# Who rounds and who takes the turned weight units in the last batch of a one-core decoder layer

## The chip, the cores and the metric

The kernel runs on one core of a Trainium2 chip. A core has TensorE (PE, with its weight loads shown apart as PEld), VectorE (DVE), ScalarE (ACT), GpSimd (POOL), SyncE (SP, whose queue here only starts transfers), one SBUF, one PSUM and 16 DMA engines. The metric is the device time of one execution in microseconds. One execution was also taken with the hardware profiler; times inside it are microseconds from the start of its span.

## The reference

One decoder layer with three parts, each added to its input: a linear self-attention, a cross-attention over 750 context rows, and a feed-forward part with ternary weights and 8-bit activations. x is 8 x 224 x 512, the context 8 x 750 x 512, and the feed-forward matrices are 2048 x 512 (gate, up) and 512 x 2048 (down).

```python
def _weight_quant(w):
    scale = 1.0 / jnp.clip(jnp.mean(jnp.abs(w)), 1e-05)
    wq = jnp.clip(jnp.round(w * scale), -1.0, 1.0) / scale
    return w + jax.lax.stop_gradient(wq - w)
def _bitlinear(x, w):
    return jnp.einsum('bsi,oi->bso', _act_quant(x), _weight_quant(w))
...
x = x + _L0_attn_ref(_layernorm(x), ...)
x = x + _L0_xattn_ref(_layernorm(x), ctx_1024, ...)   # q, k, v, softmax(q k / sqrt(32) + bias) v, projection
x = x + _L0_ffn_ref(_layernorm(x), w_gate, w_up, w_down)   # down(silu(gate(x)) * up(x))
```

So each feed-forward weight becomes -1, 0 or 1 (times one factor per matrix), and the kernel needs the three matrices turned, with the contracted index on the partitions.

## The kernel before

Three stages follow each other: self-attention for eight batches, cross-attention for eight batches, then the feed-forward part in 14 tiles of 128 rows. The change lies in the last batch (b = 7) of the cross-attention.

A batch of cross-attention has four steps s = 0..3, one for each group of four heads, and a step has 16 beats k. Each engine runs its own program in this order, and semaphores join them. In a beat of 0 to 11 PE makes the logits of one head and two key tiles (`logits`, L2024, into psS, which has two banks), and ScalarE takes their exponentials (`exponentials`, L1732, into `space`). In beats 5, 9 and 13 PE multiplies four heads' exponentials by the values (`attend`, L2067). Beside this PE makes, half by half, the logits of the next step once more for their row maxima (`maxima_half`, L2043, into psM), VectorE reduces each half (`reduce_half`, L1828), joins them (`join_maxima`, L1832), PE turns them (`turn_maxima`, L2050) and ScalarE writes them as a row of the next queries (`take_shift`, in beat 12); the next step's logits need that row. A third piece of work in each beat is a job from the table `fill` or, in the last batch, `last_fill`: projections for the next batch, and in the last batch the weights of the feed-forward part.

Those weights come in 24 units W0 to W23 of 128 x 1024 numbers (eight for each matrix). A unit has five stations:

- a load of 512 KB into a place of `f_raw` (`load_ffn`, L1509, on SP's queue; W8 to W10 by `load_freed`, L1611, on GpSimd's queue). The ten places are reused, and a load waits until the unit before it in that place is through VectorE.
- `round_weight` on ScalarE (L1723), five beats ahead of the unit's beat: f_raw * 1/mean + MAGIC, in place, which rounds to a whole number.
- `ternary` on VectorE (L1850), two beats ahead: subtract MAGIC, at most 1, to bf16 in one of three tiles `f_tern` (called xa_x_space in the trace).
- eight transposes on PE in the unit's beat (L1967) into one of three PSUM banks psR.
- `take` on VectorE in the beat after (L1792): at least -1, PSUM to the kept tile `w_all`.

The unit's beat is set by `last_fill`: W0 to W3 stand in beats 12 to 15 of step 0, W4 to W7 in step 1, W8 to W15 in step 2, W16 to W23 in step 3. GpSimd in the last batch splits the attention output in two parts when a step's division is done (`split_heads`, L1576 and L1578), stores the batch before (L1626), issues three loads (L1611) and six copies of the last keys (`pack_last_keys`, L1620), and begins the feed-forward part.

## Time and profile before

| what | value |
| --- | --- |
| three runs | 1221.86, 1225.41, 1235.33 us, median 1225.41 |
| the profiled execution | 1222.01 us, of which the span is 1220.4 us |
| mean granted clock of TensorE | 0.991 |
| busy: PE, DVE, ACT, POOL | 1165.0, 811.7, 590.3, 540.3 us |
| last batch of cross-attention | about 955 to 1035 us of the span |
| feed-forward tiles | about 1036 us to the end |

The busy shares average over stages with different limits, so the rows of the section below look at the last batch alone. A duration in a timeline row is that of the instructions named in it; where instructions follow one another closely, the next may start a tenth of a microsecond before the one ahead of it is over.

### The profile page before, as it was taken

The numbers are of one execution on the slowest core, as the hardware profiler recorded it, in microseconds if no ns is written. First come the engines' busy times: TensorE is split into PE (matmuls) and PEld (weight loads), VectorE is DVE, ScalarE is ACT, GpSimd is POOL, SyncE is SP. The second block draws the span as 40 slices with busy tenths as digits, with TensorE's granted clock in tenths as the row PEclk, the third lists the DMA queues.
The fourth block names the chain that finished last, engine by engine and source line by source line (L and its number), as shares of the span: only waits on it lengthen the run. The fifth ranks groups of instructions, "written<-read, shape, count | busy, mean of one in ns | idle before, by whom it ended". The sixth has DMA issues, their size and how long they took to land.

```text
span 1220.4 us, 25146 instructions
## 1 busy us (share of the span) xinstructions
PE 1165.0 (95%) x9483; PEld 898.7 (74%) x9483; DVE 811.7 (67%) x1494; ACT 590.3 (48%) x967; POOL 540.3 (44%) x443
## 2 busy tenths in 40 slices
PE   5899999998889999999999999999999988899996
PEld 5788888886768778887878878778788766454443
DVE  7677666667456666566665666666665588688883
ACT  4223222335245445445444444454444577588785
POOL 5021111116035666665675675765666231333240
PEclk9999999999999999999999999999999999999999
DMA  6222322425624344344343343352442685122121
GB/s 194 83 84 88 128 81 93 140 82 181 157 59 113 74 109 116 82 126 110 78 133 99 78 136 82 88 154 54 110 130 52 182 251 157 54 65 69 60 69 44
DMA packets 75252, 129.45 MB, mean 106 GB/s; under 512 B 18353, under 2 KB 34869, under 8 KB 75140
## 3 DMA queue, kind: packets, MB, share of 16 engines
q1 hardware_dynamic: 62747, 104.28, 30.9%
q0 software_dynamic: 12416, 23.96, 6.0%
q8 instruction: 59, 0.97, 0.3%
q14 instruction: 30, 0.24, 0.1%
HBM read 68.96 MB, written 11.22 MB: 66 GB/s over the span
## 4 chain that ended last, share of the span: by engine, by line
PE 82%; DVE 9%; ACT 2%; issue 2%; DMA 2%; SPq 1%; POOL 1%; DVEq 0%; ACTq 0%; POOLq 0%
PE xa_psR L2010 27%; PE sa_psR L61 14%; PE xa_psO L2067 7%; PE xa_psM L2043 7%; PE xa_psS L2024 6%; PE xa_psM L1186 4%; PE xa_psO L1204 4%; PE sa_psE L753 4%; DVE xa_m_part L1828 2%; PE xa_psS L1186 2%; DVE sa_et L509 1%; PE sa_psO L770 1%; PE xa_psO L2077 1%; DMA cv<-in_ctx_dram 1%; PE xa_psR L1195 1%
## 5 line engine op out<-in xcount | busy, mean ns | idle before, releaser
L1828 DVE TENSOR_REDUCE xa_m_part<-xa_psM 112x1 f32<-112x376 f32 x512 | 266.6, 545 | 222.6 <-PE xa_psM L2043 220.0
L1732 ACT ACTIVATE space<-xa_psS 125x448 f32<-125x448 f32 x384 | 208.6, 545 | 173.0 <-PE xa_psS L2024 171.2
L1593 POOL TENSOR_TENSOR xa_sum_space<-xa_sum_space,space 125x896 f32<-125x896 f32 x112 | 237.8, 2123 | 97.5 <-ACT space L1732 93.1
L2043 PE MATMUL xa_psM<-xa_k,xa_q 104*112 104x376 f32 x512 | 160.7, 352 | 7.2 <-DMA xa_q<-xa_q_st 2.9
L2024 PE MATMUL xa_psS<-xa_q,xa_k 104*125 104x224 f32 x768 | 146.1, 272 | 2.4 <-ACT space L1732 2.4
L2024 PEld LDWEIGHTS xa_psS<-xa_q,xa_k 104*125 104x125 f32 x768 | 137.7, 188 | 5.7 <-ACT space L1732 3.6
L2043 PEld LDWEIGHTS xa_psM<-xa_k,xa_q 104*112 104x112 f32 x512 | 87.3, 175 | 27.4 <-DVE xa_m_part L1828 9.9
L2067 PE MATMUL xa_psO<-space,cv 125*32 125x224 f32 x1536 | 94.8, 359 | 0.9 <-ACT space L1732 0.9
L1576 POOL TENSOR_SCALAR xa_oT_hi<-xa_o_f 128x224 fp32r<-128x224 f32 x32 | 25.4, 792 | 152.7 <-DVE xa_o_f L1844 152.7
L2010 PE MATMUL xa_psR<-xa_cT_hi,w_lo 128*128 128x376 f32 x256 | 91.2, 356 | 0.0
L2010 PE MATMUL xa_psR<-xa_cT_lo,w_hi 128*128 128x376 f32 x256 | 86.7, 339 | 0.0
L2010 PE MATMUL xa_psR<-xa_cT_hi,w_hi 128*128 128x376 f32 x256 | 86.4, 338 | 0.2 <-DVE xa_cT_lo L1818 0.2
L2010 PE MATMUL xa_psR<-w_hi,xa_cT_hi 128*125 128x512 f32 x192 | 79.3, 413 | 0.0
L2010 PE MATMUL xa_psR<-w_lo,xa_cT_hi 128*125 128x512 f32 x192 | 78.2, 408 | 0.0
L1593 POOL TENSOR_TENSOR xa_sum_space<-space 125x896 f32<-125x896 f32 x28 | 59.9, 2138 | 39.4 <-ACT space L1732 35.0
L2010 PE MATMUL xa_psR<-w_hi,xa_cT_lo 128*125 128x512 f32 x192 | 75.8, 395 | 0.0
L61 PE MATMUL sa_psR<-sa_xT_hi,w_hi 128*128 128x224 f32 x256 | 72.7, 284 | 2.7 <-DVE sa_xT_lo L493 2.7
L61 PE MATMUL sa_psR<-sa_xT_lo,w_hi 128*128 128x224 f32 x256 | 71.3, 279 | 0.0
L61 PE MATMUL sa_psR<-sa_xT_hi,w_lo 128*128 128x224 f32 x256 | 71.1, 278 | 0.0
L1672 ACT ACTIVATE cv<-xa_psR 125x512 f32<-125x512 f32 x48 | 28.7, 599 | 83.3 <-PE xa_psR L2010 83.3
L2067 PEld LDWEIGHTS xa_psO<-space,cv 125*32 125x32 f32 x1536 | 40.1, 109 | 30.3 <-issue 10.3
L2010 PEld LDWEIGHTS xa_psR<-xa_cT_hi,w_lo 128*128 128x128 f32 x256 | 48.7, 190 | 18.3 <-issue 18.3
(219 smaller groups left out, 2665.4 us busy)
## 6 DMA issues: line engine op xcount, KB each, us to landing
xa_k<-xa_k_st SPq DMA_DIRECT2D x378, 94.0 KB, 2.2
xa_q<-xa_q_st SPq DMA_DIRECT2D x192, 56.0 KB, 2.0
cv<-in_L_ffn_w_gate_dram SPq DMA_DIRECT2D x14, 512.0 KB, 4.9
cv<-in_ctx_dram POOLq DMA_DIRECT2D x7, 1000.0 KB, 12.0
cv<-in_L_ffn_w_down_dram SPq DMA_DIRECT2D x10, 512.0 KB, 7.1
cv<-in_L_ffn_w_up_dram SPq DMA_DIRECT2D x9, 512.0 KB, 6.0
sa_x_raw<-in_x_dram SPq DMA_DIRECT2D x8, 448.0 KB, 7.4
sa_rows<-in_x_dram SPq DMA_DIRECT2D x8, 448.0 KB, 3.8
```

Source lines behind the costliest of these rows:

```text
L61: ins = nc.tensor.matmul(out, left(i, c), right(j, c), start=first and n == 0, stop=last and n == len(terms) - 1)
L753: last = M.matmul(psE[0:T, j, cols], k_rot[own, g, c, t * T:(t + 1) * T], q_rot[own, g, c, t * T:N], start=c == 0, stop=c == 1)
L1186: last = M.matmul(bank[c % 2], xq_T[:, k], gu_T[w][c // 2][:, k, c % 2 * CW:(c % 2 + 1) * CW], start=k == 0, stop=k == KT - 1)
L1204: last = M.matmul(psY[:], hq_T[:, k], down_T[half][:, m], start=k == 0, stop=k == IT - 1)
L1593: nc.gpsimd.tensor_tensor(p_sum[:], before, tile, ALU.add).then_inc(p_summed, 1)
L1672: return nc.scalar.activation(out, in_, ACT.Copy, scale=scale)
L1732: nc.scalar.activation(pT[:, (s + i) % 2, j], psS[0:KB, (HG * i + j) % EXP_BANKS, 0:2 * N], ACT.Exp).then_inc(exp_done, 1)
L1828: V.tensor_reduce(m_part[:, t, jj, seg:seg + 1], psM[0:T, seg, 0:SEG], AX.X, ALU.max).then_inc(mx_read, 1)
L2010: last = M.matmul(out, left(i, k), right(j, k), start=m == 0, stop=m == len(terms) - 1)
L2024: last = M.matmul(psS[0:KB, (HG * i + j) % EXP_BANKS, a * N:(a + 1) * N], k4[0:ROWS, s % 2, j, col:col + KB], q4[0:ROWS, s, j, :], start=T ...
L2043: M.matmul(psM[0:T, seg, 0:SEG], q4[0:ROWS, g, jj, t * T:(t + 1) * T], k4[0:ROWS, g % 2, jj, seg * SEG:(seg + 1) * SEG], start=True, stop= ...
L2067: last = M.matmul(psO[HD * j:HD * (j + 1), col:col + N], weights, pT[:, (s + i) % 2, j, a * N:(a + 1) * N], start=t == 0 and col == 0, sto ...
```

## The change

Three things change, all in the last batch. GpSimd rounds W0 to W15 (`round_weight` moves there for them, as one tensor_scalar with multiply and add), at points between its other duties; ScalarE keeps W16 to W23, and waits once until all 16 are rounded. ScalarE takes the odd units W1, W3, ..., W15 out of PSUM with the function Sign, where VectorE took them with a maximum. And VectorE's `ternary` for a unit whose third predecessor is one of those waits until PE has turned that predecessor, since the tile `f_tern` is about to be written again.

```diff
+    POOL_ROUNDS, SPLIT_BEAT, LATER = 16, 4, 8
...
+        def by_scalar(what):
+            return int(what[1:]) < POOL_ROUNDS and int(what[1:]) % 2 == 1
...  (GpSimd)
+            def round_weight(unit):
+                n = weight_of(unit)[0]
+                r = raw_of[unit]
+                if unit == 0:
+                    pool.wait_ge(w_scale_step, 3)
+                if unit in FREED:
+                    wait_apart(pool, f_freed, len(FREED) * DMA, pool_passed)
+                else:
+                    wait_apart(pool, f_in[r], DMA * (raw_use[unit] + 1), pool_passed)
+                nc.gpsimd.tensor_scalar(f_raw[r], f_raw[r], w_inv[:, n:n + 1], MAGIC, ALU.mult, ALU.add).then_inc(f_rounded, 1)
+            def round_weights(first, end):
+                for unit in range(POOL_ROUNDS):
+                    if first <= unit_beat[unit] - ROUND_AHEAD < end:
+                        round_weight(unit)
...
+                    if b == B - 1:
+                        round_weights(BEATS * (s - 1) + LATER, BEATS * s + SPLIT_BEAT)
                     if (b, s) != (0, 0):
                         split_heads(*((b, s - 1) if s > 0 else (b - 1, NG - 1)))
...
                         load_freed()
+                        round_weights(BEATS + SPLIT_BEAT, BEATS + LATER)
                         pack_last_keys()
+                    elif b == B - 1:
+                        round_weights(BEATS * s + SPLIT_BEAT, BEATS * s + LATER)
...  (ScalarE, take)
-                if what[0] in "YW":
+                if what[0] == "Y" or what[0] == "W" and not by_scalar(what):
                     return
                 act.wait_ge(full[r], use_of[what, b])
+                if what[0] == "W":
+                    dst = turned_place(what)
+                    nc.scalar.activation(dst, src.bitcast(BF16).rearrange("p (k c) -> p k c", k=dst.shape[1]),
+                                         ACT.Sign).then_inc(read[r], 1)
+                    return
...  (ScalarE, round_weight)
-                if unit == 0:
+                if unit == POOL_ROUNDS:
                     act.wait_ge(const_made, 5)
                     act.wait_ge(w_scale_step, 3)
+                    act.wait_ge(f_rounded, POOL_ROUNDS)
...
-                            for unit in range(UNITS_W):
+                            for unit in range(POOL_ROUNDS, UNITS_W):
...  (VectorE, take and ternary)
+                    if by_scalar(what):
+                        return
...
+                if unit >= 3 and by_scalar(f"W{unit - 3}"):
+                    before = (f"W{unit - 3}", B - 1)
+                    dve.wait_ge(full[bank_of[before]], use_of[before])
```

The first place is ScalarE from beat 9 of step 2 into step 3. Exponentials are written to `space`, roundings to `cv`, `xa_c_space` and `xa_q_st_space`, the maxima's row to `xa_q`. Before:

```order
486 L1723 ACTIVATE cv<-cv,xa_magic,xa_w_inv 128x1024
487 L1732 ACTIVATE space<-xa_psS 125x448 x2
488 L1723 ACTIVATE cv<-cv,xa_magic,xa_w_inv 128x1024
489 L1672 ACTIVATE xa_q<-xa_psM 4x896
490 L1723 ACTIVATE cv<-cv,xa_magic,xa_w_inv 128x1024
491 L1723 ACTIVATE xa_c_space<-xa_c_space,xa_magic,xa_w_inv 128x1024 x3
492 L1732 ACTIVATE space<-xa_psS 125x448 x2
493 L1723 ACTIVATE xa_c_space<-xa_c_space,xa_magic,xa_w_inv 128x1024
```

And with the change, the same place:

```order
468 L1723 ACTIVATE w_all<-xa_psR 128x4x256
469 L1771 ACTIVATE space<-xa_psS 125x448
470 L1762 ACTIVATE cv<-cv,xa_magic,xa_w_inv 128x1024
471 L1708 ACTIVATE xa_q<-xa_psM 4x896
472 L1762 ACTIVATE cv<-cv,xa_magic,xa_w_inv 128x1024
473 L1762 ACTIVATE xa_c_space<-xa_c_space,xa_magic,xa_w_inv 128x1024 x2
474 L1723 ACTIVATE w_all<-xa_psR 128x4x256
475 L1762 ACTIVATE xa_c_space<-xa_c_space,xa_magic,xa_w_inv 128x1024
476 L1771 ACTIVATE space<-xa_psS 125x448 x2
477 L1762 ACTIVATE xa_c_space<-xa_c_space,xa_magic,xa_w_inv 128x1024
```

The rounding of W15 (486) is gone, the taking of W13 has come in (468), and the taking of W15 (474) now stands between the roundings of W19 and W20, ahead of the first exponentials of step 3. There is no table load in either piece.

The second place is GpSimd's program for steps 1 and 2 of the last batch, with the change; before, only the rows of L1590, L1592, L1640, L1625 and L1634 stood there (as L1576, L1578, L1626, L1611 and L1620).

```order
234 L1652 TENSOR_SCALAR cv<-cv,xa_w_inv 128x1024
235 L1590 TENSOR_SCALAR xa_oT_hi<-xa_o_f 128x224
236 L1592 TENSOR_TENSOR xa_oT_lo<-xa_o_f,xa_oT_hi 128x224
237 L1640 DMA x_dram<-xa_x_res 112x2x512
238 L1625 DMA xa_c_space<-in_L_ffn_w_up_dram 128x2x512 x3
239 L1652 TENSOR_SCALAR cv<-cv,xa_w_inv 128x1024 x2
240 L1634 DMA xa_k<-xa_k_st 32x752 x6
241 L1652 TENSOR_SCALAR xa_c_space<-xa_c_space,xa_w_inv 128x1024 x5
242 L1590 TENSOR_SCALAR xa_oT_hi<-xa_o_f 128x224
243 L1592 TENSOR_TENSOR xa_oT_lo<-xa_o_f,xa_oT_hi 128x224
244 L1652 TENSOR_SCALAR xa_q_st_space<-xa_q_st_space,xa_w_inv 128x1024
```

Row 234 is W5 (W0 to W4 stand ahead of it), 239 is W6 and W7, 241 is W8 to W12, and 244 is W13, with W14 and W15 behind it. The three loads stand behind W5, and the six key copies behind W6 and W7.

## Rows read from the trace of the kernel before

**Rows 1.** The page: span, and busy time of each engine.

```profile
span 1220.4 us, 25146 instructions
PE 1165.0 (95%) x9483; PEld 898.7 (74%) x9483; DVE 811.7 (67%) x1494; ACT 590.3 (48%) x967; POOL 540.3 (44%) x443
```

**Rows 2.** Windows: stretch length; busy us (instructions); PEclk; DMA share; GB/s. Sum: 985 to 1030.

```profile
980.00:985.00 5.00, 5.00 (x53) 3.95 (x51) 3.52 (x7) 4.12 (x7) 2.95 (x3) 1.00 0.02 5
...
1000.00:1005.00 5.00, 3.72 (x49) 2.53 (x48) 4.97 (x10) 3.99 (x7) 1.69 (x2) 1.00 1.04 337
...
1010.00:1015.00 5.00, 3.91 (x61) 2.94 (x57) 4.88 (x11) 3.91 (x5) 0.00 (x0) 1.00 1.07 303
1015.00:1020.00 5.00, 3.19 (x52) 2.30 (x44) 4.30 (x8) 4.97 (x6) 0.00 (x0) 1.00 1.10 355
1020.00:1025.00 5.00, 4.72 (x44) 4.34 (x48) 4.96 (x8) 5.00 (x8) 1.70 (x2) 0.66 0.15 51
...
sum 45.00, PE 37.66 PEld 28.72 DVE 40.85 ACT 35.17 POOL 9.72; mean PE 4.18 PEld 3.19 DVE 4.54 ACT 3.91 POOL 1.08
```

**Rows 3.** Timeline of ScalarE: start, us, line, operation; in brackets idle time and releaser.

```profile
964.50 1.23 ACT L1723 ACTIVATE cv<-cv,xa_magic,xa_w_inv 128x1024 f32<-128x1024 f32 x1
...
1009.69 1.23 ACT L1723 ACTIVATE cv<-cv,xa_magic,xa_w_inv 128x1024 f32<-128x1024 f32 x1
...
1014.23 0.91 ACT L1672 ACTIVATE xa_q<-xa_psM 4x896 fp32r<-4x896 f32 x1
...
1016.31 3.49 ACT L1723 ACTIVATE xa_c_space<-xa_c_space,xa_magic,xa_w_inv 128x1024 f32<-128x1024 f32 x3
1019.70 0.95 ACT L1732 ACTIVATE space<-xa_psS 125x448 f32<-125x448 f32 x2
...
1024.80 0.97 ACT L1732 ACTIVATE space<-xa_psS 125x448 f32<-125x448 f32 x2
```

**Rows 4.** Timeline of PE, about the boundary of steps 2 and 3.

```profile
1013.58 0.35 PE L2050 MATMUL xa_psM<-ident,xa_m_neg 112*4 112x112 f32 x2 [1.09 <-DVE xa_m_neg L1832]
...
1020.28 0.47 PE L2024 MATMUL xa_psS<-xa_q,xa_k 104*125 104x224 f32 x2 [1.61 <-ACT space L1732]
```

**Rows 5.** GpSimd groups, forms apart: busy us, mean ns; then idle before and releasers.

```profile
L967 POOL TENSOR_SCALAR xa_k_st_space<-xa_sum_space,ff_x_mv,ff_x_rs 128x512 f32<-128x512 f32 x14 | 29.3, 2090 | 2.8 <-POOL ff_x_rs L961 2.6 <-issue 0.2
...
L973 POOL TENSOR_SCALAR xa_k_st_space<-xa_k_st_space,ff_x_scale 128x512 f32<-128x512 f32 x14 | 9.7, 691 | 22.4 <-issue 20.9 <-DVE ff_x_scale L1080 1.5
...
L959 POOL TENSOR_SCALAR ff_x_ve<-ff_x_mv 128x1 f32<-128x1 f32 x14 | 3.2, 231 | 9.1 <-DVE ff_x_mv L1067 8.8 <-POOL xa_oT_lo L1578 0.2
```

**Rows 6.** ScalarE, a group of the feed-forward part, same columns.

```profile
L1012 ACT ACTIVATE xa_c_space<-xa_psR 128x1024 bf16<-128x1024 bf16 x28 | 28.5, 1016 | 0.3
```

**Rows 7.** VectorE, groups of the stretch 955 to 1035, same columns.

```profile
L1792 DVE TENSOR_SCALAR w_all<-xa_psR 128x1024 bf16<-128x1024 bf16 x24 | 16.1, 683 | 1.8 <-PE xa_psR L1967 1.8
```

**Rows 8.** Timeline of GpSimd in the last batch.

```profile
982.18 1.44 POOL L1578 TENSOR_TENSOR xa_oT_lo<-xa_o_f,xa_oT_hi 128x224 fp32r<-128x224 f32 x1
...
985.11 2.37 POOL L1611 DMA_DIRECT2D xa_c_space<-in_L_ffn_w_up_dram  x3 [0.46 <-PE xa_psR L2010]
992.40 3.15 POOL L1620 DMA_DIRECT2D xa_k<-xa_k_st  x6 [4.93 <-PE xa_psS L2024]
1001.26 1.02 POOL L1576 TENSOR_SCALAR xa_oT_hi<-xa_o_f 128x224 fp32r<-128x224 f32 x1 [5.72 <-DVE xa_o_f L1844]
...
1023.52 0.66 POOL L1578 TENSOR_TENSOR xa_oT_lo<-xa_o_f,xa_oT_hi 128x224 fp32r<-128x224 f32 x1
```

**Rows 9.** Timeline of VectorE: two `ternary` that overlap a GpSimd instruction.

```profile
982.41 0.68 DVE L1850 TENSOR_SCALAR xa_x_space<-xa_xn 128x1024 bf16<-128x1024 f32 x1
...
1023.92 0.81 DVE L1850 TENSOR_SCALAR xa_x_space<-xa_c_space 128x1024 bf16<-128x1024 f32 x1
```

**Rows 10.** The load of W20: issue (ns), and us from issue to landing.

```profile
L1509 SPq DMA_DIRECT2D xa_c_space<-in_L_ffn_w_down_dram x1: 1402/1402/1402, 1006.7 to 1006.7; - x1
...
DMA to landing us min/median/max: 10.9/10.9/10.9
```

More of the change, by code:

```diff
@@ L1424, in cross_attention, with turned_place @@
         w_totalled, w_scale_step = sem("w_totalled"), sem("w_scale_step")
+        def by_scalar(what):
+            return int(what[1:]) < POOL_ROUNDS and int(what[1:]) % 2 == 1
+        def turned_place(what):
+            n, t = weight_of(int(what[1:]))
+            kept = place(n, t // (TURNS // 2))
+            t = t % (TURNS // 2)
+            if n < 2:
+                return kept.rearrange("p (k i) -> p k i", k=KT)[:, :, 2 * t * P:2 * (t + 1) * P]
+            return kept.rearrange("p (k d) -> p k d", d=D)[:, 2 * t:2 * t + 2]
         def ffn_part(unit):
@@ L1715, in round_weight @@
                 r = raw_of[unit]
-                if unit == 0:
+                if unit == POOL_ROUNDS:
                     act.wait_ge(const_made, 5)
                     act.wait_ge(w_scale_step, 3)
-                if unit in FREED:
-                    act.wait_ge(f_freed, len(FREED) * DMA)
-                else:
-                    act.wait_ge(f_in[r], DMA * (raw_use[unit] + 1))
+                    act.wait_ge(f_rounded, POOL_ROUNDS)
+                act.wait_ge(f_in[r], DMA * (raw_use[unit] + 1))
                 nc.scalar.activation(f_raw[r], f_raw[r], ACT.Identity, bias=magic[:, 0:1], scale=w_inv[:, n:n + 1]).then_inc(f_rounded, 1)
@@ L1783, in take @@
                 if what[0] == "W":
-                    n, t = weight_of(int(what[1:]))
-                    kept = place(n, t // (TURNS // 2))
-                    t = t % (TURNS // 2)
-                    if n < 2:
-                        dst = kept.rearrange("p (k i) -> p k i", k=KT)[:, :, 2 * t * P:2 * (t + 1) * P]
-                    else:
-                        dst = kept.rearrange("p (k d) -> p k d", d=D)[:, 2 * t:2 * t + 2]
+                    if by_scalar(what):
+                        return
+                    dst = turned_place(what)
                     dve.wait_ge(full[r], use_of[what, b])
```

## The prediction

> **What bounds the kernel now.** I read the page first, then the windows of the last batch, then the timelines of ScalarE and PE at the boundary of steps 2 and 3, and last the landing times of the loads. The page shows PE busy for 95% of the span [rows 1], but that is an average over stages, and this change touches only the 80 us from 955 to 1035.
>
> The windows divide that stretch in three. Up to 985, PE is busy for all of each window (5.00 of 5.00 [rows 2]): it still has projections and maxima of the last keys to do, and nothing that ScalarE, VectorE or GpSimd save there can move the end. From 985 to 1030 PE is busy for 37.66 of 45 us [rows 2], so all that any change to the other engines could win is about 7.3 us of idle PE, plus what a low clock costs. VectorE is the fullest of the helpers there, 40.85 of 45 us, 91% [rows 2]. And from 1000 to 1020 the 16 DMA engines are at a share of 1.04 to 1.10, and at 0.15 behind it [rows 2]: the loads of the last units saturate them until about 1020.
>
> At the boundary of steps 2 and 3 the chain lies on ScalarE. It writes the maxima's row at 1014.23, after PE had waited 1.09 us for VectorE's joined maxima (1013.58 [rows 4]); then come the rounding of W17, three roundings from 1016.31 for 3.49 us (W18, W19, W20), and only then the first two exponentials of step 3, at 1019.70 [rows 3]. PE waits 1.61 us for them (1020.28 [rows 4]) and the granted clock of the window from 1020 to 1025 is 0.66, a mixture of the level of 2.4 GHz and that of 1.2 GHz [rows 2]. The full clock that is lacking in it is 0.34 x 5 = 1.7 us.
>
> How much can this chain be advanced? W20's load was issued at 1006.7 and landed 10.9 us later, at 1017.6 [rows 10]. Its rounding began when two of the three from 1016.31 were done: (3.49 - 1.23) / 2 = 1.13 us from start to start, so at 1018.57 [rows 3]. That is 1.0 us behind its data. Since the DMA engines are full, the data doesn't come sooner because an engine asks sooner. So **1.0 us is the floor of the gain** at this place, whatever VectorE and GpSimd do before it.
>
> **The change part by part.**
>
> *ScalarE loses 16 roundings.* At 1.13 us from start to start, 18.1 us. W0 to W5 stand before 985 or at its edge, where PE is full, and are worth nothing. Those of W6 to W15 stood between exponentials of steps 1 and 2. They free ScalarE, which was busy for 3.99 and 3.91 of 5 us in the windows from 1000 and from 1010 [rows 2]; what PE waits for there is VectorE's maxima [rows 4], so I count this at nothing. The cover is VectorE's 91%: were VectorE emptier, the relief would count, and this is in the third rival.
>
> *GpSimd gains them.* No row shows this size. The nearest is the rounding of the feed-forward rows, L973: the same two operations (times a value for each partition, plus a constant), f32 to f32, 512 numbers, 0.691 us, 14 times. An instruction of one number takes 0.231 us (L959), so 512 numbers cost 0.46 and 1024 cost 0.231 + 2 x 0.46 = 1.15 us. The other end is L967, with two values for each partition, 2.090 us for 512, which gives 0.231 + 2 x 1.86 = 3.95 us [rows 5]. I take **1.15**, because L973 has the very operations and operands, and L967 has others. In all 16 x 1.15 = 18.4 us on an engine that has the time: W0 could start at 964.5, as on ScalarE [rows 3]; W6 and W7 (2.3 us) fit in the 4.93 us that GpSimd idled before the key copies at 992.40, so neither these nor the three loads at 985.11 are late [rows 8]. The tight part is W8 to W15. The key copies end at 995.55, and ScalarE was done with W15 at 1009.69 + 1.23 = 1010.92 [rows 3, 8]. Between lie 15.4 us; less one split of 1.02 + 0.66 [rows 8] that is 13.7 us for eight roundings, so GpSimd keeps pace up to **1.7 us** each. At 1.15 it is 9.2 us, and what holds it then is the landing of the loads, as it did ScalarE. The new wait of ScalarE for all 16 falls after 1010.92, when they are done: nothing.
>
> *ScalarE gains eight takes.* The copy of a bank of the same shape takes 1.016 us (L1012 [rows 6]); I take that for Sign too. The order of the change shows no table load among them. Seven stand in the time that the roundings leave. The eighth, W15's, stands ahead of the rounding of W20, in the chain: **+0.9 us** (1.02 less the tenth by which neighbours overlap), with 0 as the lower end if ScalarE waits for data there anyway, and 1.0 as the upper.
>
> *VectorE loses eight takes* of 0.68 us [rows 7]. Those of W1 and W3 lie before 985, and those of W13 and W15 behind the joined maxima. Four (W5, W7, W9, W11) lie in the stretch that leads to them: 2.7 us at most, 0 if each falls into a wait for PE. VectorE was idle for 9% of that stretch, mostly in its first half; I take two thirds, **-1.8 us**.
>
> *VectorE's ternaries now run beside GpSimd's roundings.* A ternary takes 0.68 us (982.41 [rows 9]); the one at 1023.92, beside a GpSimd instruction that ran to 1024.18, took 0.81, or 0.13 more [rows 8, 9]. The instruction beside the ternary at 982.41 took 1.44 instead of 0.66 us [rows 8]. So both pay something. Seven ternaries (W8 to W14) lead to the maxima: 7 x 0.13 = **+0.9 us**. The ends are 0, and one whole rounding for each, 7 x 1.15 = 8.1 us. I take the row.
>
> The Trainium skill, in "SBUF — State Buffer", section "Who interferes with whom", says that VectorE in a 2-port mode and GpSimd share a pair of ports, and that "whoever issues first gets the shared pair for the whole instruction", while the other stands still. By that rule the upper end would be the rule and not the exception. The trace agrees in part: 0.78 us on GpSimd's side is more than a whole ternary, but 0.13 us on VectorE's side is less than the 0.26 us that were left of GpSimd's instruction.
>
> *VectorE's new wait* (the third predecessor turned) asks for an event that its own take waited for before: nothing.
>
> **The sum.** The maxima's row comes 1.8 - 0.9 = 0.9 us sooner, W15's take puts 0.9 us back, and W20's rounding begins at about 1018.6 as before: **no change**. Behind it ScalarE, PE and the feed-forward part do what they did. Against the profiled execution's own 1222.01 us (span 1220.4) that is 1222.0. The median of the runs, 1225.41, is 3.4 us above it, with no edit; a median of new runs may lie anywhere between. I give 1223.5, half way.
>
> **The rivals.**
>
> 1. *The ternaries wait for whole roundings.* GpSimd rounds W8 to W12 back to back, and each ternary is released by the end of one rounding, just as the next one starts. For: the 0.78 us [rows 8]. Against: the 0.13 us [rows 9], and that loads space the roundings out. VectorE is at 91%, so nearly all of it would count. At half a rounding for each of seven: 4.0 instead of 0.9, +3.1 us, 1225 on the profiled scale; at a whole one: +7.2, 1229. It decides from about 0.4 us for each ternary. Chance 0.16.
>
> 2. *GpSimd rounds at L967's pace* and becomes the bound; slower. Eight roundings from 964.5 are 31.6 us, with the 3.8 us of 982.18 and 985.11 [rows 8] 999.9 instead of 992.40, so the key copies are 7.5 us late; eight more end at 995.55 + 7.5 + 1.7 + 31.6 = 1036.4 instead of 1010.9: +25 us, 1247. It decides above 1.7 us for each. Against it stands L973, with all 14 at the same size. Chance 0.06.
>
> 3. *A gain to the floor, and the clock with it.* If the freed ScalarE and all four takes count, the chain comes forward by the 1.0 us that the loads allow; and if PE's wait of 1.61 us goes and with it the stretch at 1.2 GHz, 1.7 more: -2.7 us, 1219.3. Against it: the loads hold the exponentials, not PE, so a PE that arrives sooner waits longer. Chance 0.16.
>
> **How the numbers follow.** Forecast 0.62, rivals 0.16, 0.06, 0.16. The range takes in rival 3 with 2 us for the scatter of runs, 1217, and rival 1 up to its upper end with 2 us, 1231; rival 2 stays out. One per cent is 12 us, about what a measurement of this kernel can tell from no change. Idle PE and low clock in the stretch are 7.3 + 1.7 = 9 us together, so faster by over 1% would need something that I don't see: 0.02. Slower by over 1% is rival 2 and the tail of rival 1: 0.08. Within 1%: 0.90.
>
> **What would show it.** GpSimd's roundings at 1.1 to 1.4 us, and W15's done before 1010. Eight takes on ScalarE of about 1.0 us and no table load. The first exponential of step 3 at 1019.7 within 1 us, with W20's rounding less than 1 us behind its landing. Ternaries of 0.68 to 0.85 us; ones above 1 us speak for rival 1. A granted clock of 1.00 from 1020 to 1025 speaks for rival 3. The forecast is wrong if the exponentials of step 3 move by more than 2 us, or if the loads of W16 to W23 are issued at a quite different time, since the floor hangs on them.

## The result: 0.3% slower, where no change was forecast

| | before | with the change |
| --- | --- | --- |
| median of 20 runs each | 1225.79 us (1221.86 to 1235.33) | 1229.51 us (1225.47 to 1236.09) |
| ratio, 95% interval | | 1.0032 [1.0016, 1.0048], or +3.9 us |
| profiled execution, its span | 1222.01, 1220.4 us | 1228.35, 1226.7 us |
| mean granted clock | 0.991 | 0.985 |

The time lies inside the forecast range (1217 to 1231) and within 1% of before, but the difference is real: the interval leaves out 1. The forecast of no change was wrong by about 4 us. The number that it gave, 1223.5, lies 6.0 us below the median; 2.3 of them are before's own median.

**A mark to count from.** The profiled span grew by 6.3 us, and 2.9 of that have nothing to do with the change: GpSimd's split of the attention output (L1576, now L1590) that opens the last batch began at 958.39 before and at 961.32 after, with the same code ahead of it. In thirteen profiled executions of this study, whatever the kernel, this *opening split* (the "mark" below) falls between 958.4 and 962.6. So two profiles are compared here by times after their own opening split. From it to the end it is 262.01 us before and 265.38 after: +3.4 us, which agrees with the +3.9 us of the timed runs.

| us after the opening split | before | after |
| --- | --- | --- |
| the maxima's row written in step 1 | 35.71 | 35.71 |
| the maxima's row written in step 2 | 55.84 | 58.82 |
| first exponential of step 3 | 61.31 | 65.20 |
| first ff_x_ve on GpSimd (the feed-forward part begins) | 70.53 | 75.85 |
| end of the span | 262.01 | 265.38 |

Up to step 1 nothing moves, which is what the prediction said of the stretch where PE is full. Step 2 loses 2.98 us, the boundary to step 3 0.91, step 3 itself 1.43, and the feed-forward part gives 1.95 back. Page of the changed kernel, to be held against [rows 1]:

```profile
span 1226.7 us, 25146 instructions
PE 1166.8 (95%) x9457; PEld 901.9 (74%) x9483; DVE 808.8 (66%) x1486; ACT 580.6 (47%) x959; POOL 560.1 (46%) x459
```

The work moved as meant: GpSimd has 16 instructions and 20 us more, ScalarE and VectorE eight fewer each. The price of each moved instruction, in the groups of the stretch (busy us, mean ns; then idle before):

```profile
L1652 POOL TENSOR_SCALAR xa_c_space<-xa_c_space,xa_w_inv 128x1024 f32<-128x1024 f32 x5 | 5.6, 1120 | 3.4 <-DMA xa_c_space<-in_L_ffn_w_up_dram 3.4
L1723 ACT ACTIVATE w_all<-xa_psR 128x1024 bf16<-128x1024 bf16 x8 | 8.1, 1020 | 3.3 <-PE xa_psR L2005 3.3
```

1.12 us against 1.15 forecast, and 1.020 against 1.016. Neither a slow GpSimd nor the take's price is the cause. Windows of the changed kernel (columns as in [rows 2]; step 2 ends in the fourth of those shown, and the boundary to step 3 lies in the fifth):

```profile
1000.00:1005.00 5.00, 3.37 (x20) 2.95 (x20) 4.97 (x7) 2.10 (x5) 3.00 (x3) 0.79 1.04 268
1005.00:1010.00 5.00, 4.03 (x39) 2.86 (x43) 4.22 (x8) 1.95 (x3) 3.29 (x4) 0.53 1.05 371
1010.00:1015.00 5.00, 4.92 (x58) 3.79 (x53) 4.23 (x9) 2.89 (x5) 4.01 (x3) 1.00 1.09 283
...
1020.00:1025.00 5.00, 3.62 (x60) 2.61 (x52) 3.36 (x6) 4.95 (x6) 0.00 (x0) 1.00 0.75 249
1025.00:1030.00 5.00, 2.90 (x21) 2.77 (x21) 4.12 (x6) 5.00 (x7) 1.69 (x2) 0.68 0.01 2
1030.00:1035.00 5.00, 5.00 (x54) 3.50 (x53) 3.19 (x5) 2.71 (x6) 0.00 (x0) 0.64 0.02 3
```

The clock column is what differs most from [rows 2]. From 1000 to 1010 the granted clock is 0.79 and 0.53, where it was 1.00 before: for most of this stretch PE works at 1.2 GHz. It falls again behind the boundary, 0.68 and 0.64 in two windows, where before it was one window of 0.66. What comes ahead of the first fall is on VectorE and GpSimd. Timeline of VectorE, changed kernel:

```profile
999.61 1.01 DVE L1863 TENSOR_REDUCE xa_m_part<-xa_psM 112x1 f32<-112x376 f32 x2 [2.43 <-PE xa_psM L2081]
1000.53 1.90 DVE L1888 TENSOR_SCALAR xa_x_space<-xa_c_space 128x1024 bf16<-128x1024 f32 x1
```

And GpSimd, changed kernel:

```profile
998.56 3.32 POOL L1652 TENSOR_SCALAR xa_c_space<-xa_c_space,xa_w_inv 128x1024 f32<-128x1024 f32 x3
1002.30 1.12 POOL L1652 TENSOR_SCALAR xa_c_space<-xa_c_space,xa_w_inv 128x1024 f32<-128x1024 f32 x1 [0.42 <-DMA xa_c_space<-in_L_ffn_w_up_dram]
```

The ternary of W8, 0.68 or 0.69 us in every profile in which GpSimd doesn't round beside it, takes 1.90 here. GpSimd runs three roundings without a gap from 998.56 to 1001.88. The ternary begins at 1000.53, inside the second, whose end is at 998.56 + 2 x 1.10 = 1000.76, and it is over at 1002.43: 0.55 us behind the end of the third. So it wasn't let in at the end of the second rounding, though the third began only after it; it had to wait for the end of that one, behind which GpSimd itself waited for a load (0.42). PE's timeline shows who waited:

```profile
1002.58 0.77 PE L2005 MATMUL xa_psR<-xa_ident_b,xa_x_space 128*128 128x128 bf16 x8 [1.27 <-DVE xa_x_space L1888]
...
1005.97 1.01 PE L2005 MATMUL xa_psR<-xa_ident_b,xa_x_space 128*128 128x128 bf16 x8 [1.12 <-DVE xa_x_space L1888]
...
1019.01 0.35 PE L2088 MATMUL xa_psM<-ident,xa_m_neg 112*4 112x112 f32 x2 [1.09 <-DVE xa_m_neg L1867]
...
1027.10 0.76 PE L2062 MATMUL xa_psS<-xa_q,xa_k 104*125 104x224 f32 x2 [3.30 <-ACT space L1771]
```

At 1002.58 PE has waited 1.27 us for this ternary. The eight transposes of a unit then take 1.01 us where they take 0.61 at full clock (in e6, below), and 1.12 us of waiting for W9 follow. At the other end, PE waits 3.30 us ahead of the logits of step 3, against 1.61 in [rows 4]. ScalarE there, in the changed kernel:

```profile
1020.14 0.91 ACT L1708 ACTIVATE xa_q<-xa_psM 4x896 fp32r<-4x896 f32 x1
1021.07 1.24 ACT L1762 ACTIVATE cv<-cv,xa_magic,xa_w_inv 128x1024 f32<-128x1024 f32 x1
1022.22 2.36 ACT L1762 ACTIVATE xa_c_space<-xa_c_space,xa_magic,xa_w_inv 128x1024 f32<-128x1024 f32 x2
1024.48 1.00 ACT L1723 ACTIVATE w_all<-xa_psR 128x1024 bf16<-128x1024 bf16 x1
1025.39 1.23 ACT L1762 ACTIVATE xa_c_space<-xa_c_space,xa_magic,xa_w_inv 128x1024 f32<-128x1024 f32 x1
1026.52 0.95 ACT L1771 ACTIVATE space<-xa_psS 125x448 f32<-125x448 f32 x2
```

From the row to the first exponentials ScalarE has no gap, before [rows 3] and after. Before it is four roundings, 5.47 us; now the take at 1024.48 stands among them, 6.38 us. So this term is the +0.9 us that was forecast for it. A second take stands in this chain a little earlier, W13's, ahead of the rounding of W16 and of the row; e4 shows what it costs.

Last, the part given back. Beyond the last batch, some 96 us after the opening split, the profile of before has a fall of the clock in the feed-forward part, and that of the change has none. Window of before, and then of the changed kernel:

```profile
1054.39:1058.39 4.00, 4.00 (x17) 2.05 (x18) 3.18 (x8) 2.39 (x4) 1.37 (x2) 0.57 0.29 70
```

```profile
1057.32:1061.32 4.00, 3.27 (x15) 1.29 (x14) 2.38 (x9) 2.58 (x3) 1.49 (x3) 1.00 0.37 117
```

The experiments show that this is not the change's merit.

### The profile page after: what moved, and what is told of

Read it like the earlier page. It is cut to its first block, busy times and chain, and to the rows that moved or that the text cites. A ratio compares the mean times of both kernels' runs of the same rounds, so it can differ in the third digit from the quotient of the medians.

```text
span 1226.7 us, 25146 instructions
## 1 busy us (share of the span) xinstructions
PE 1166.8 (95%) x9457; PEld 901.9 (74%) x9483; DVE 808.8 (66%) x1486; ACT 580.6 (47%) x959; POOL 560.1 (46%) x459
## 4 chain that ended last, share of the span: by engine, by line
PE 82%; DVE 9%; ACT 2%; issue 2%; DMA 2%; SPq 1%; POOL 1%; DVEq 0%; ACTq 0%; POOLq 0%
PE xa_psR L2048 27%; PE sa_psR L61 14%; PE xa_psO L2105 8%; PE xa_psM L2081 7%; PE xa_psS L2062 6%; PE xa_psM L1186 4%; PE xa_psO L1204 4%; PE sa_psE L753 4%; DVE xa_m_part L1863 2%; PE xa_psS L1186 2%; DVE sa_et L509 1%; PE sa_psO L770 1%; PE xa_psO L2115 1%; DMA cv<-in_ctx_dram 1%; PE xa_psR L1195 1%
## 5 line engine op out<-in xcount | busy, mean ns | idle before, releaser
L1590 POOL TENSOR_SCALAR xa_oT_hi<-xa_o_f 128x224 fp32r<-128x224 f32 x32 | 25.5, 797 | 122.0 <-DVE xa_o_f L1879 122.0
```

## The experiments

Four causes were to be told apart: roundings on GpSimd holding VectorE back, the takes on ScalarE, W15's take among them, and the clock that falls behind waits. All times are us after the opening split of the same profile. "Turn" is PE's turning of step 2's joined maxima (1013.58 in [rows 4]), "row" is the maxima's row of step 2, "exp" the first exponential of step 3, "ffx" the first ff_x_ve. "Fall at 96" tells whether the clock fell there, in the feed-forward part.

| kernel | turn | row | exp | ffx | end | ternary of W8 | fall at 96 | ratio to before, 95% |
| --- | --- | --- | --- | --- | --- | --- | --- | --- |
| before | 55.19 | 55.84 | 61.31 | 70.53 | 262.01 | 0.68 | yes | |
| the change | 57.69 | 58.82 | 65.20 | 75.85 | 265.38 | 1.90 | no | 1.0032 [1.0016, 1.0048] |
| e1_round_only | 55.42 | 56.07 | 61.55 | 70.79 | 262.20 | 0.80 | yes | 1.0003 [0.9982, 1.0024] |
| e2_sign_only | 55.35 | 56.97 | 63.35 | 73.32 | 265.06 | 0.69 | yes | 1.0010 [0.9988, 1.0032] |
| e3_no_sign15 | 59.90 | 61.02 | 66.50 | 77.81 | 268.01 | 2.99 | no | 1.0014 [0.9994, 1.0034] |
| e4_apart | 55.33 | 56.47 | 62.84 | 73.13 | 265.02 | 0.69 | yes | 1.0019 [0.9999, 1.0038] |
| e5_after_again | 56.51 | 57.64 | 64.02 | 75.04 | 265.13 | 1.03 | no | a single run |
| e6_apart_no15 | 55.33 | 56.45 | 61.93 | 72.64 | 262.27 | 0.68 | no | 0.9992 [0.9972, 1.0012] |
| e7_before_fill | 56.18 | 56.82 | 62.30 | 71.27 | 261.33 | 0.68 | no | 1.0002 [0.9979, 1.0024] |
| e8_apart_fill | 56.48 | 57.61 | 64.00 | 72.98 | 264.62 | 0.68 | yes | 1.0016 [0.9996, 1.0037] |
| e9_before_fills | 55.20 | 55.85 | 61.33 | 70.30 | 261.98 | 0.68 | yes | 0.9989 [0.9972, 1.0005] |
| e10_after_fills | 55.81 | 56.79 | 63.17 | 72.15 | 261.81 | 1.02 | no | 1.0019 [0.9997, 1.0040] |
| e11_round_apart_fills | 55.31 | 55.96 | 61.44 | 70.42 | 261.99 | 0.69 | yes | 0.9987 [0.9968, 1.0006] |

### e1_round_only: the roundings on GpSimd alone

```diff
         def by_scalar(what):
-            return int(what[1:]) < POOL_ROUNDS and int(what[1:]) % 2 == 1
+            return False
```

> GpSimd rounds W0 to W15 as in the change, but VectorE takes all units out of PSUM as before. Theory P (a ternary waits for whole GpSimd roundings, PE idles and drops to 1.2 GHz): the ternary of W8 again takes about 1.9 us beside the roundings of W9 and W10, and the time is about 3 us (0.25%) over the kernel before, only 0.9 us below the change. Theory S (the loss is ScalarE's new takes): the time is that of the kernel before, ratio 1.000.

Measured: ratio 1.0003 [0.9982, 1.0024]. The row comes 0.23 us later than before, and from the row on nothing differs by more than 0.04 us up to the feed-forward part. VectorE, and below it GpSimd, in this kernel:

```profile
1001.49 0.80 DVE L1888 TENSOR_SCALAR xa_x_space<-xa_c_space 128x1024 bf16<-128x1024 f32 x1
```

```profile
999.53 4.85 POOL L1652 TENSOR_SCALAR xa_c_space<-xa_c_space,xa_w_inv 128x1024 f32<-128x1024 f32 x4
```

The ternary began 0.24 us ahead of a rounding's end (999.53 + 2 x 1.10 = 1001.73), and got in there: it ended at 1002.29. GpSimd's next rounding waited instead, since four take 4.85 us here where 4.42 would do. This is the forecast 0.13 us, in the kernel's one profile. It follows that rounding on GpSimd needn't cost anything, and also that it gains nothing: 18 us taken off ScalarE don't bring the row forward.

### e2_sign_only: the takes on ScalarE alone

```diff
-    POOL_ROUNDS, SPLIT_BEAT, LATER = 16, 4, 8
+    POOL_ROUNDS, SPLIT_BEAT, LATER = 0, 4, 8
...
         def by_scalar(what):
-            return int(what[1:]) < POOL_ROUNDS and int(what[1:]) % 2 == 1
+            return int(what[1:]) < 16 and int(what[1:]) % 2 == 1
```

ScalarE rounds all 24 units again, each behind its own load.

> ScalarE rounds all units as before and takes the odd units W1 to W15 with Sign; GpSimd rounds none. Theory P: no ternary over 0.8 us; ScalarE has 8 more instructions, W15's in its chain, so 1 to 2 us over the kernel before (ratio 1.001). Theory S: the whole loss of the change, about 4 us, or more, since ScalarE is not relieved of roundings (ratio 1.003 or more).

Measured: 1.0010 [0.9988, 1.0032]; row +1.13, row to exp 6.38 instead of 5.47, exp to ffx 9.97 instead of 9.22. No ternary waits here and the clock of step 2 is 1.00, yet the profile is 3.05 us longer than before from mark to end. In this profile the takes are thus a cost of their own: 1.13 us in step 2, 0.91 from W15's, and 0.75 behind the exponentials. Of the first, 0.16 us lie ahead of PE's turn of the maxima and 0.98 between turn and row, where ScalarE works without a gap from 1013.64 until it writes the row at 1019.61. Twice as much as in e4 below, where the roundings up to W15 are gone from ScalarE. The timed ratio agrees with either of the two theories to within its interval.

### e3_no_sign15: VectorE keeps W15's take

```diff
-            return int(what[1:]) < POOL_ROUNDS and int(what[1:]) % 2 == 1
+            return int(what[1:]) < POOL_ROUNDS - 2 and int(what[1:]) % 2 == 1
```

ScalarE still takes W1, W3, ..., W13.

> The change, but W15 is taken by VectorE again, so no Sign stands between the roundings of W19 and W20. Both theories: W20's rounding starts 0.9 us sooner after the row of maxima than in the change. Theory P: 0.9 to 1 us below the change (ratio 1.0025 against before), the ternary of W8 stays at 1.9 us. Theory S: the loss goes almost wholly, ratio 1.001 or less.

Measured: 1.0014 [0.9994, 1.0034]. From the row to the exponential it is 5.48 us, so the 0.9 us are gone, and PE's wait ahead of the logits of step 3 is 2.09 us instead of 3.30. But this profile has the worst step 2 of all, the row at 61.02. VectorE and GpSimd:

```profile
998.78 2.99 DVE L1888 TENSOR_SCALAR xa_x_space<-xa_c_space 128x1024 bf16<-128x1024 f32 x1
```

```profile
996.82 4.40 POOL L1652 TENSOR_SCALAR xa_c_space<-xa_c_space,xa_w_inv 128x1024 f32<-128x1024 f32 x4
```

The ternary lost twice: it stood from 998.78 until GpSimd's run of four was over at 1001.22, and ended 0.55 us behind that. With 2.3 us lost on VectorE the clock fell deeper than in the change, in windows:

```profile
1000.00:1005.00 5.00, 2.52 (x14) 2.28 (x14) 4.97 (x6) 1.16 (x3) 2.35 (x4) 0.61 1.03 303
1005.00:1010.00 5.00, 4.32 (x39) 2.94 (x43) 3.69 (x7) 1.53 (x3) 4.68 (x4) 0.50 1.09 352
```

The code up to this ternary is that of the change, and so is its place: 39.2 us after the opening split in both. So 1.90 and 2.99 are outcomes of the same race, and one profile of a kernel doesn't tell its mean.

### e4_apart: GpSimd steps aside for the ternaries

Two roundings wait until VectorE has made a ternary, so that they can't run back to back over W8's.

```diff
                 n = weight_of(unit)[0]
                 r = raw_of[unit]
+                if unit in (9, 11):
+                    pool.wait_ge(f_tern_ready, {9: 9, 11: 10}[unit])
```

> The change, but GpSimd begins the rounding of W9 only when W8's ternary is done, and W11's only when W9's is. Theory P: no ternary over 0.9 us at W8, PE waits under 0.8 us there, the granted clock stays at 1.00 in step 2, and the time falls by 1.2 us (the port alone) to 3 us (with the clock), to a ratio of 1.0008 to 1.0022 against before. Theory S, or a theory by which step 2 is late because GpSimd's split stands ahead of W13's rounding: no change against the change, ratio 1.003.

Measured: W8's ternary 0.69 us, clock 1.00 throughout step 2, row at 56.47 instead of 58.82. Timed 1.0019 [0.9999, 1.0038]. The race is gone from the profile, and 0.6 us of the row's delay remain, as do the 0.9 us of W15 (6.37). Where the 0.6 us arise, ScalarE and PE of this kernel show:

```profile
1014.93 1.02 ACT L1725 ACTIVATE w_all<-xa_psR 128x1024 bf16<-128x1024 bf16 x1
...
1016.28 1.24 ACT L1764 ACTIVATE cv<-cv,xa_magic,xa_w_inv 128x1024 f32<-128x1024 f32 x1
1017.55 0.91 ACT L1710 ACTIVATE xa_q<-xa_psM 4x896 fp32r<-4x896 f32 x1
```

```profile
1016.41 0.35 PE L2090 MATMUL xa_psM<-ident,xa_m_neg 112*4 112x112 f32 x2 [1.08 <-DVE xa_m_neg L1869]
```

PE has turned the maxima at 1016.76, but ScalarE is in W16's rounding until 1017.52, since W13's take at 1014.93 stood ahead of it. From turn to row it is 1.14 us, where before has 0.65 (1013.58 to 1014.23 [rows 3, 4]). So 0.5 of the 0.6 us are W13's take on ScalarE. VectorE's side, the turn, is at 55.33: later than before (55.19) and not sooner, with four takes fewer on VectorE ahead of it. In every profile with W13's take on ScalarE turn to row is 0.98 to 1.63 us, in every one without it 0.65. What is left of the difference comes after the row, on PE and in the windows:

```profile
1024.50 0.76 PE L2064 MATMUL xa_psS<-xa_q,xa_k 104*125 104x224 f32 x2 [3.30 <-ACT space L1773]
```

```profile
1020.00:1025.00 5.00, 1.52 (x15) 1.19 (x12) 4.53 (x7) 5.00 (x7) 0.00 (x0) 0.84 0.74 244
1025.00:1030.00 5.00, 5.00 (x40) 4.34 (x42) 3.92 (x7) 5.00 (x7) 1.69 (x2) 0.50 0.01 3
```

PE is busy for 1.52 of 5 us and then works a whole window at 1.2 GHz.

### e5_after_again: the change, once more

The kernel is the change, not edited.

> The changed kernel once more, one look. In the first look the ternary of W8 began 39.2 us after the split that opens the last batch and took 1.90 us, while the same ternary at the same place took 0.80 and 2.99 us in two neighbours. Theory P1 (who gets the port is chance at this point): the place of all marks up to 36 us is the same to 0.1 us, but that ternary takes one of 0.8, 1.9 or 3.0 us, perhaps another than before. Theory P2 (the order of the change decides it): 1.90 us again and the maxima's row 58.8 us after the split.

Measured: 1229.32 us, row at 57.64, and this ternary:

```profile
1001.77 1.03 DVE L1888 TENSOR_SCALAR xa_x_space<-xa_c_space 128x1024 bf16<-128x1024 f32 x1
```

It began 0.46 us ahead of a rounding's end and got in there, as in e1. Step 2 still lost 1.80 us: 1.32 up to the turn, where the clock fell all the same, and 0.48 behind it. So the same program gives 1.03 or 1.90 us for the same instruction at the same place.

### e6_apart_no15: e4 and e3 together

The edits of e3 and of e4.

> The change with both repairs: GpSimd waits for W8's ternary before W9 and for W9's before W11, and W15 is taken by VectorE. If port and Sign of W15 are the loss: the maxima's row 56.5 us after the split (before 55.8), first exponential of step 3 at 62.0 (before 61.3, the change 65.2, the repair of the port alone 62.8), ratio 1.000 to 1.001 against before. If the takes on ScalarE cost in themselves: ratio 1.002 or more.

Measured: 0.9992 [0.9972, 1.0012], an interval that lies wholly below the change's: the loss is gone with GpSimd still rounding 16 units and ScalarE still taking seven. Row to exp is 5.48 us. Beside e4 it is the cleanest pair of the study, rows at 56.45 and 56.47: the exponentials come 0.91 us sooner. The end is 2.75 us sooner, but 2.26 of that lie beyond ffx, where e4 has the fall at 96 and e6 hasn't, so only 0.49 us of the 0.91 are still there when the feed-forward part begins. The rest went to the low clock, which is as long here as in e4, though W15's take isn't there:

```profile
1023.74 0.76 PE L2064 MATMUL xa_psS<-xa_q,xa_k 104*125 104x224 f32 x2 [2.09 <-ACT space L1773]
```

```profile
1020.00:1025.00 5.00, 2.42 (x25) 2.03 (x22) 4.85 (x7) 5.00 (x6) 0.00 (x0) 0.85 0.98 318
1025.00:1030.00 5.00, 5.00 (x42) 4.03 (x43) 4.71 (x8) 4.22 (x7) 1.69 (x2) 0.50 0.00 1
```

### e7_before_fill and e8_apart_fill: small matmuls in PE's wait

Six of them in before, twelve in e4_apart, into a bank that is not in use, ahead of the logits of step 3:

```diff
+                        if (b, s, k) == (B - 1, NG - 1, 2):
+                            for _ in range(6):
+                                M.matmul(psM[:, 1, 0:P], ident[:], ident[:], start=True, stop=True)
```

> The kernel before with six idle multiplications of 128 x 128 on PE (about 0.2 us each, into a bank that nobody uses then) in beat 2 of step 3, where PE waits 1.61 us for an exponential. Theory C (a wait of this length costs again through the clock): the exponential stays where it is (61.3 us after the split), the granted clock of the stretch is 1.00 instead of 0.79, and the feed-forward part begins 1 to 1.7 us sooner. Against C: the clock falls anyway or the marks don't move.

> The change with GpSimd held apart from the ternaries of W8 and W9, and 12 such multiplications in beat 2 of step 3, where PE waited 3.30 us. Theory C: first exponential of step 3 at 62.8 us after the split as without them, clock 1.00 in the next 8 us, and the feed-forward part begins at about 71.8 us instead of 73.1; what then is left against before (70.5) is the Sign of W15 (0.9) and 0.6 of step 2. Against C: 73.1 again.

Measured: 1.0002 [0.9979, 1.0024] and 1.0016 [0.9996, 1.0037]. The aim was reached: the clock stays at 1.00 through the boundary, and from exp to ffx it is 8.97 and 8.98 us. That prices the low clock there, as 9.22 - 8.97 = 0.25 us in before, 10.29 - 8.98 = 1.31 in e4 and, since e10 below also has 8.98, 10.65 - 8.98 = 1.67 in the change and 2.04 in e5. e6 and e3, which lack W15's take, were not run with the fill; 8.98 gives an estimate for them, 1.73 and 2.33. But both kernels lost a microsecond of step 2 to something else. Up to step 3 the code of e7 is that of before, and the code of e8 that of e4. The windows from 37 to 43 and from 43 to 47 us after the opening split, first of before and e7, then of e4 and e8:

```profile
995.39:1001.39 6.00, 4.40 (x42) 3.06 (x32) 4.70 (x8) 5.73 (x7) 0.28 (x2) 1.00 1.07 264
1001.39:1005.39 4.00, 3.58 (x52) 2.61 (x53) 4.00 (x9) 2.99 (x6) 1.56 (x2) 1.00 1.01 359
```

```profile
997.97:1003.97 6.00, 4.34 (x42) 3.12 (x32) 4.70 (x8) 5.90 (x8) 0.28 (x2) 1.00 1.07 267
1003.97:1007.97 4.00, 3.58 (x43) 2.25 (x43) 4.00 (x8) 2.60 (x5) 1.56 (x2) 0.72 1.02 351
```

```profile
998.08:1004.08 6.00, 4.08 (x44) 3.10 (x32) 4.69 (x8) 3.22 (x6) 3.55 (x4) 1.00 1.06 269
1004.08:1008.08 4.00, 3.57 (x55) 2.75 (x55) 3.95 (x8) 1.74 (x3) 3.51 (x2) 1.00 1.04 356
```

```profile
997.68:1003.68 6.00, 4.07 (x44) 3.10 (x32) 4.69 (x8) 3.21 (x6) 3.57 (x4) 1.00 1.04 275
1003.68:1007.68 4.00, 3.57 (x43) 2.34 (x43) 3.45 (x7) 1.46 (x2) 3.62 (x2) 0.70 1.04 354
```

In each pair the first windows are nearly alike (the largest difference is ScalarE's 5.73 against 5.90), and in the second the clock of one is 1.00 and that of the other 0.72 or 0.70. In the first pair PE's wait just ahead of the fall differs, 0.82 us in before and 1.24 in e7; in the second it doesn't, 1.94 in e4 and 1.95 in e8. Their rows follow: 55.84 against 56.82, 56.47 against 57.61. So this fall belongs to no kernel; the same code gets it in some executions, with no lost race ahead of it.

### e9_before_fills, e10_after_fills and e11_round_apart_fills: fill at three places

Small matmuls ahead of the transposes of W8 and W9, in step 3, and in the feed-forward part. e9 is before with them, e10 the change (twelve in step 3), e11 the roundings alone, kept apart as in e4.

```diff
+                    for _ in range({8: 4, 9: 5}.get(unit, 0)):
+                        M.matmul(out[:, 0:P], ident[:], ident[:], start=True, stop=True)
                     pe.wait_ge(f_tern_ready, unit + 1)
...
+            for _ in range(7):
+                M.matmul(psY[:], ident[:], gu_T[0][0][:, 0, 0:CW], start=True, stop=True)
```

> The kernel before with idle multiplications on PE wherever it waited long: 4 and 5 of 128 x 128 ahead of the transposes of W8 and W9 (0.8 us of wait each), 6 in beat 2 of step 3, and 7 of 128 x 512 before the feed-forward loop. Theory C (the granted clock falls in PE's waits, by chance in step 2, and each fall costs 1 to 2 us): clock 1.00 from 36 to 110 us after the split, maxima's row at 55.8, end about 260 us after the split instead of 262.0; ratio 0.999, hardly to be told from 1. Against C: the clock falls in spite of it.

> The change with the same work added (12 in beat 2 of step 3, where its wait is longer). Theory C: clock 1.00 all through; the maxima's row between 56.5 and 57.5 us after the split, by how long W8's ternary waits for the port (0.1 to 1.1 us); the exponential 6.4 us after that row as in the change (W15's take is still there); the feed-forward part 9.0 us behind it instead of 10.7; end about 262.5 instead of 265.4, ratio 1.000 to 1.001. Against C: end at 264 or more.

> GpSimd's roundings alone (VectorE takes all units), held apart from the ternaries of W8 and W9, and the added work on PE. If port, W15's take and clock are all of the loss: the row of maxima at 55.9 to 56.5, the exponential 5.5 us behind it, end at 260 to 261 us after the split, as the kernel before with the added work, ratio 0.999 to 1.000.

Measured: 0.9989 [0.9972, 1.0005], 1.0019 [0.9997, 1.0040] and 0.9987 [0.9968, 1.0006]. In the profiles the clock of step 2 is 1.00 in all three, and from exp to ffx it is 8.97, 8.98 and 8.98 us. e10 is e9 with the change: row +0.94, of which 0.61 lie ahead of the turn (W13's ternary, which met a rounding that had just begun, took 1.61 instead of 0.69) and 0.33 behind it, on ScalarE; and +0.9 for W15. Windows of e10, of step 2:

```profile
1000.00:1005.00 5.00, 4.59 (x46) 4.38 (x46) 4.97 (x8) 1.99 (x4) 2.98 (x3) 1.00 1.05 277
1005.00:1010.00 5.00, 4.42 (x59) 3.31 (x58) 4.61 (x9) 3.24 (x5) 4.57 (x3) 1.00 1.06 374
```

The fill in the feed-forward part did nothing: e9 and e11 have the fall at 96 and e10 hasn't, and e9 and e11 end at 262.0, not at the 260 to 261 expected. Over all profiles, from ffx to the end it is 191.41 to 191.89 us with that fall (before, e1, e2, e4, e8, e9, e11) and 189.53 to 190.20 without it (the change, e3, e5, e6, e7, e10). Before's code is on both sides (e7 has it there), so the 1.95 us that the change gave back in its profile are chance. None of the kernels is faster than before beyond its interval. With medians of 1224.55 against 1226.57 for before beside it, e9 and e11 (1225.64) may be a microsecond or two better; the runs don't settle that.

## Why the forecast was wrong

**The step that failed** is "*VectorE's ternaries now run beside GpSimd's roundings*", priced at 7 x 0.13 = +0.9 us, together with "*VectorE loses eight takes*", priced at -1.8 us, and the sentence that seven of ScalarE's takes "*stand in the time that the roundings leave*". The first two made a gain of 0.9 us, which was to pay for W15's take. In the profile of the change step 2 made a loss of 2.98 instead: 2.50 up to PE's turn of the maxima, and 0.48 behind it, on ScalarE. The lost takes brought nothing, one ternary lost 1.2 us to GpSimd, W13's take cost 0.48, and the clock, which had no term, fell. The two signs that the forecast named for its own failure are both there: a ternary above 1 us, and exponentials of step 3 that move by more than 2 us (3.9 from the mark).

- *The ternaries.* The mechanism was that of rival 1, but with a large loss at one place and not at seven, and by chance. Whether a ternary that finds GpSimd rounding gets in at the end of that rounding (0.80 us in e1, 1.03 in e5, 1.02 in e10) or only behind one or two more (1.90 in the change, 2.99 in e3) differs between executions of the same code. The forecast took 0.13 us from one row in which GpSimd had nothing behind its instruction [rows 8, 9], and such a row can't show a queue. The Trainium skill, in "SBUF — State Buffer", section "Who interferes with whom", says that whoever issues first holds the shared ports for the whole instruction. The traces agree for the rounding under way at W8: in none of the five did the ternary get in before its end. They don't for the rest. In the change and in e3 roundings that began 0.24 us and more after the ternary went first, and in e1, with the same order of starts, the ternary did. And ternaries can pass a rounding that began well before them, GpSimd (first) and VectorE in e10:

```profile
1005.35 3.02 POOL L1654 TENSOR_SCALAR xa_c_space<-xa_c_space,xa_w_inv 128x1024 f32<-128x1024 f32 x1 [2.38 <-DMA xa_c_space<-in_L_ffn_w_up_dram]
1005.72 0.68 DVE L1890 TENSOR_SCALAR xa_x_space<-xa_c_space 128x1024 bf16<-128x1024 f32 x1
...
1006.78 0.69 DVE L1890 TENSOR_SCALAR xa_x_space<-xa_c_space 128x1024 bf16<-128x1024 f32 x1
```

  So who pays at a meeting, and how much, is open in these traces.
- *The takes that VectorE lost.* The working was: two thirds of 2.7 us. PE's turn of the maxima, which waits for VectorE, comes at 55.33 in e4 and e6 without these takes, and at 55.31 and 55.42 in e11 and e1 with them: nothing gained. The groups of the last batch show where they went. Before, VectorE's reductions had waited for PE this long (first fence), and after the change this long (second fence; the takes of [rows 7] are in it too):

```profile
L1828 DVE TENSOR_REDUCE xa_m_part<-xa_psM 112x1 f32<-112x376 f32 x45 | 23.4, 544 | 10.0 <-PE xa_psM L2043 9.9
```

```profile
L1863 DVE TENSOR_REDUCE xa_m_part<-xa_psM 112x1 f32<-112x376 f32 x45 | 23.4, 543 | 14.3 <-PE xa_psM L2081 14.2
L1827 DVE TENSOR_SCALAR w_all<-xa_psR 128x1024 bf16<-128x1024 bf16 x16 | 10.9, 685 | 3.9 <-PE xa_psR L2005 3.8
```

  The takes fell from 16.1 to 10.9 us, -5.2, and the waits for PE rose by 4.3 and 2.0. So VectorE, busy for 91%, was not the bound here. The forecast also said that PE waits for VectorE's maxima in that stretch, and cited one wait for it; in before's profile, from 994 to 1014.5, PE waits 3.1 us, of which 1.5 for maxima, 0.8 for a ternary and 0.8 for exponentials.
- *The take of W13.* It was counted among the seven that cost nothing. It stands ahead of W16's rounding, which ScalarE kept, and that one ahead of the row: 0.48 us in the change and in e4, by turn to row. W15's was not the only take in the chain.
- *The clock in step 2* had no term. The forecast read 1.00 in [rows 2] as a property of the place. It was luck: with before's code e7 lost 1.0 us to it, with e4's code e8 1.1 us. Both profiles of the change itself had the fall, and with the lost race it was deeper (row at 58.82, and 57.64 in e5 where the race was won). The ternary's 1.2 us and the fall are in the 2.50 up to the turn; how much of the fall that wait causes can't be split from one profile.

**W15's take: right.** +0.9 forecast. The six profiles with it have 6.37 to 6.39 us from row to exponential, the seven without it 5.47 to 5.48.

**What follows the two takes in the chain: missed.** PE's wait ahead of the logits of step 3 is 1.61 us in before and e1, 2.09 with W13's take on ScalarE (e3, e6), and 3.30 with W15's too. The low clock behind the wait costs 0.25 us in before and 1.0 to 2.3 in the six profiles with a longer wait and no fill (for e2, e3 and e6 by the estimate with 8.98). It isn't W15's take that decides this: e6 and e3 have 1.73 and 2.33 without it. No kernel had VectorE keep W13 and W15 alone, so that W13's part isn't tested by itself. Rival 3 counted 1.7 us as what before loses there; taking the low clock away in e7 gave 0.25. The full clock that is lacking in a window is not the time that it costs: in e7 PE has short waits of 0.2 to 0.3 us for ScalarE and VectorE behind the exponentials, where before, at the low clock, it has none over 0.2.

**Right, and without effect:** GpSimd's price (1.12 for 1.15) and pace, though W15's rounding ended at 1014.01, 52.7 us after the mark, as 52.5 before (the sign "before 1010" was set below the 1010.92 that the forecast read for before itself); no table load for Sign; 18 us of roundings off ScalarE worth nothing (e1: 1.0003); the loads issued 46.2 us after the mark, 45.9 before. The 1.0 us floor was never tested, since no kernel brought the row forward.

**The sum, redone for the change's profile:** step 2, boundary, step 3 and the rest are 2.98 + 0.91 + 1.43 - 1.95 = +3.4 us; for e5's, 1.80 + 0.91 + 1.80 - 1.39 = +3.1. Of the timed ratios, those of e6, e9 and e11 lie wholly below the change's interval. So the loss is gone when both the meeting at W8 and W15's take are taken away (e6). Those of e1, e2, e3, e4, e7, e8 and e10 hold 1 but reach into it, so that by their times alone no half of the change can be named as the one at fault. W15's 0.9 us is in every profile that has its take, and in none without. **What stays open** is how often W8's ternary loses its race and how often the clock falls in step 2: the one profile of e10 is as short as before's from mark to end, 261.81, while its timed median is 0.19% longer. The +3.9 us of the timed runs are thus not divided among the causes.

## What to carry to other kernels

An engine that is busy for 91% need not be the bound: price work taken off it by what it waits for next. Before giving GpSimd back-to-back instructions beside VectorE's, price each meeting with up to the rest of GpSimd's run, and not with one overlap, or keep them apart by a wait. Look for every operation that the change puts ahead of an instruction in the chain, not only for the last one: here W13's take cost 0.48 us and W15's 0.91. Behind the longer wait came a longer stretch at 1.2 GHz, which cost as much again or more (1.0 to 2.3 us).

## What the runs showed of the hardware

- A VectorE instruction of 0.68 us (f32 to bf16, 128 x 1024) that meets GpSimd's 1.12 us instructions in a run ended 0.55 to 0.57 us behind the end of one of them in all five profiles where W8's does: the first end in e1, e5 and e10, the next in the change, the one after that in e3. In the last two that end was also the end of GpSimd's run.
- GpSimd's roundings get longer beside ternaries, too, and the ternaries then needn't: the rounding at 1011.07 took 1.85 instead of 1.12 us, with one ternary beside it, and that of W12 in e10 took 3.02, with two of 0.68 and 0.69.
- Whether the granted clock falls at a place with waits of 1 to 2 us differs between executions of the same code; a fall cost 1.0 to 1.1 us in step 2 (e7, e8), and from ffx on the profiles with a fall at 96 are 1.2 to 2.4 us longer than those without, 1.8 on the average. Six small matmuls in a wait of 1.6 us, or twelve in one of 3.3, kept it at 1.00.
- GpSimd's tensor_scalar of 1024 f32 numbers per partition, times a value for each partition plus a constant, takes 1.12 us, and 512 take 0.69; Sign from PSUM on ScalarE (128 x 1024 bf16) takes 1.020 us, and no table load appears beside the exponentials.
